# Cross attention: the exponentials cast to f16 and transposed by DMA, and their sums taken from a column of ones

## The chip, the cores and the metric

One core of one Trainium2 chip runs the whole kernel. The core's engines are TensorE (PE in the profile; PEld is its weight load), VectorE (DVE), ScalarE (ACT), GpSimd (POOL) and SyncE (SP), which only issues transfers here. The metric is device time in microseconds (us), from the launch of the program to its end; the profile's span runs from the first to the last instruction. Less is better.

## What is computed

The input `x` has 4 sequences of 2048 positions and 512 features, `ctx` 4 sequences of 128 positions. Three blocks follow each other, each as `x + block(layernorm(x))`:

```python
x = x + _L0_attn_ref(_layernorm(x), ...)    # 16 heads; attention over the 4 sequences of one position
x = x + _L0_xattn_ref(_layernorm(x), ctx_1024, ctx_1024, mask, ...)
x = x + _L0_ffn_ref(_layernorm(x), ...)
```

The change concerns the second one, cross attention with 16 heads of 32 features:

```python
scores = jnp.einsum('bnlh,bnph->bnlp', qm, km) / np.sqrt(HEAD_DIM)
scores = jnp.where(mask, scores, MASK_FILL)
attn = jax.nn.softmax(scores, axis=-1)
out = jnp.einsum('bnlp,bnph->bnlh', attn, vm)
return out @ Wo.T + bo
```

The third block, in the kernel a hinge function on a projection to 64 gates and a product back to 512 features, is interleaved with it. Inputs and outputs are f32.

## The kernel before

The program has two stages. `first_block` runs self attention over the positions and prepares the context: keys, mask and values go to memory in the form that the second stage reads. `cross_block` does cross attention and the third block. An f32 product is made from two parts, a high and a low one: ScalarE copies the source to the narrower type (high), VectorE subtracts this from the source (low), and TensorE multiplies high by high, high by low and low by high (`PASSES`). For the values' product the parts are f16, elsewhere `F32R`.

The cross stage has 16 steps (`step(j, p)`, run by `run_steps`) of 512 rows. A step has four tiles of 128 rows, numbered t = 0 to 3, and then the products that belong to all 512 rows: `ffn_in` for the step before and `queries` for the step to come. Each engine has its own hand-written order of work in its `step`, and semaphores tie them together; no scheduler moves anything. The work is staggered: in tile t TensorE computes the scores of tile t, but the values, the output projection and the rest belong to tiles one to three earlier.

One tile's way through attention, with the names of the code:

- `scores(t)` on TensorE: 4 products with `ones` and `fillrows` for the mask, 48 with the queries and `kt`, into the four banks `sc`.
- `tops(t, g)` on VectorE: the negative maximum of each head into `ntop`, four heads (one g) at a time.
- `exps(t, g)` on ScalarE: one exponential for each head into `prob` (f32, `prob_c` in the profile), with the head's sum by `accum_out`, which the profile shows as a second instruction, ACTIVATION_READ_ACCUMULATOR.
- `prob_T(i)` on TensorE: four heads of `prob` transposed into a bank of the ring; `prob_hi` and `prob_lo` on ScalarE and VectorE take the high and low part into `pT` (f16).
- `values(t)` on TensorE, a tile later: 48 products of `pT` with `v_c`, 32 columns each.
- `normalise(t)` on VectorE: the reciprocal of the sums and `attn` = values times reciprocal.
- `attn_T`, `attn_hi`, `attn_lo`: `attn` transposed, high and low part into `aT`.
- `out_proj(t)` on TensorE with `wo`; `add_attn(t)` on VectorE adds the residual `xr` into `x2`; `statistics(t)` takes mean and variance (`mv`, `vare`).
- `norm2(j, t)` on GpSimd: `rstd`, the normalised rows `xn2` and the addition of `bf`; then `norm2_T`, `norm2_hi`, `norm2_lo` into `x2T`, `ffn_in`, the hinges `g_sb`, the gates `gT` and `ffn_out`.

Beside this, GpSimd normalises the next step's rows (`norm(i)`, which waits for the load of `x1`) and adds the bias to the residual (`residual(i)`).

Transposes and most products write to a ring of four PSUM banks. `slot_turns` lists who takes a bank, in the order of TensorE's work, and `bank_before` gives the turn four places earlier, which must have been emptied (`taken`) before the bank is used again. SyncE's queue holds the loads of `x1`, of the rows of `kt`, `fillrows` and `v_c`, and the stores of the output.

## Time and profile before

| | |
|---|---|
| median of 3 runs | 1782.91 us (1781.09 to 1783.93) |
| the profiled execution | 1784.44 us |
| its span | 1782.6 us |
| PE busy | 1685.4 us (95%) |
| PEld busy | 1392.6 us (78%) |
| DVE busy | 1514.8 us (85%) |
| ACT busy | 1069.8 us (60%) |
| POOL busy | 1017.6 us (57%) |
| mean granted clock of TensorE | 0.983 |
| DMA | 98.75 MB, mean 55 GB/s |

The profiled execution takes 1.5 us more than the median. Around its span there are 1.8 us. The self stage fills the span up to about 844 us, the cross stage the rest. Busy times are sums over stages with different limits, so the table alone doesn't tell what holds a step. In the rows by stretch the columns are the length, then busy time and count of PE, PEld, DVE, ACT and POOL, the granted clock (1.00 is full), the DMA engines' busy share and GB/s; in the rows of a timeline they are the start, the duration, engine, line, operation with output and inputs, and in brackets the idle time before and what ended it. The rows are taken from one step in the middle of the cross stage (about 1206 to 1263 us), from its first tiles, and, for shapes that the cross stage doesn't have, from the self stage.

### The profile page before, as it was taken

What the parts mean: (1) busy time and instruction counts of PE and PEld (TensorE: products, weight loads), DVE (VectorE), ACT (ScalarE), POOL (GpSimd) and SP (SyncE); (2) the same over time, 40 slices, a digit from 0 to 9 for tenths busy, and PEclk for the clock granted to TensorE, in tenths of its full rate; (3) what the DMA queues carried; (4) which work ended last, traced back from release to release, by engine and by line L of the source; (5) the groups of instructions that cost most, each with busy time, mean ns of one, the idle gap of its engine ahead of it and who ended that gap; (6) DMA issues with size and microseconds to landing.
All of it is one profiled execution on the core that took longest, in us unless ns stands there. A gap on an engine that the chain in (4) does not pass through costs nothing.

```text
span 1782.6 us, 37666 instructions
## 1 busy us (share of the span) xinstructions
PE 1685.4 (95%) x13824; PEld 1392.6 (78%) x13824; DVE 1514.8 (85%) x2089; ACT 1069.8 (60%) x3420; POOL 1017.6 (57%) x721
## 2 busy tenths in 40 slices
PE   6899999999999999997799999999999999999996
PEld 5678888888888888885677787778777787777874
DVE  6788888888888888787678898888988899888886
ACT  4434444444443334442767788777877788777884
POOL 3267766666666666695554464545654465544521
PEclk9999999999999999998799999999999999999998
DMA  5410111111111111044201112011111112011101
GB/s 210 128 42 25 47 48 48 47 47 47 47 47 47 47 47 47 2 107 79 68 8 51 62 62 63 25 62 62 63 38 43 62 62 69 19 62 62 39 20 54
DMA packets 72793, 98.75 MB, mean 55 GB/s; under 512 B 22208, under 2 KB 30528, under 8 KB 72640
## 3 DMA queue, kind: packets, MB, share of 16 engines
q1 hardware_dynamic: 72064, 96.63, 17.0%
q8 instruction: 97, 1.59, 0.4%
q14 instruction: 56, 0.46, 0.1%
q10 hardware_dynamic: 576, 0.07, 0.0%
HBM read 59.66 MB, written 37.03 MB: 54 GB/s over the span
## 4 chain that ended last, share of the span: by engine, by line
PE 28%; ACT 12%; DVE 8%; issue 4%; DVEq 0%; POOL 0%; ACTq 0%; POOLq 0%
PE ring L1464 11%; ACT prob_c L1679 10%; DVE g_sb L1794 5%; PE sc L1492 5%; PE ring L1504 3%; PE ring L1469 3%; PE ring L1549 3%; PE sc L1484 2%; PE sc L1464 1%; DVE q_first L1975 1%; ACT relu L1660 1%; DVE g_sb L1791 1%; DVE gT L1803 1%; ACT gT L1669 1%; ACT pT L1648 0%
## 5 line engine op out<-in xcount | busy, mean ns | idle before, releaser
L447 PE MATMUL qb<-wqkv,xT 128*128 128x512 f32 x2304 | 551.9, 393 | 6.1 <-DVE wqkv L1016 6.1
L447 PEld LDWEIGHTS qb<-wqkv,xT 128*128 128x128 f32 x2304 | 429.7, 189 | 93.7 <-DVE wqkv L1016 6.3
L1679 ACT ACTIVATE prob_c<-sc,ntop 128x128 f32<-128x128 f32 x1024 | 362.6, 390 | 22.1 <-DVE ntop L1821 18.7
L1410 POOL TENSOR_TENSOR rstd<-vare,half_c 128x1 f32<-128x1 f32 x64 | 35.1, 549 | 433.6 <-DVE vare L1875 433.6
L1679 ACT ACTIVATION_READ_ACCUMULATOR prob_c<-sc,ntop 128x1 f32 x1024 | 236.1, 231 | 0.0
L352 POOL TENSOR_TENSOR prod_pool<-v,prob 128x1024 f32<-128x1024 f32 x64 | 179.9, 2810 | 67.8 <-DVE prob L911 62.6
L1464 PE MATMUL ring<-wqkv,aT_c 128*128 128x512 f32 x768 | 194.5, 402 | 8.0 <-DVE aT_c L1778 7.1
L663 ACT ACTIVATE v<-qb 128x512 f32<-128x512 f32 x64 | 38.3, 598 | 259.9 <-PE qb L447 249.6
L583 PE MATMUL ob<-wout,aT 128*128 128x512 f32 x768 | 191.4, 398 | 0.8 <-DVE aT L941 0.8
L1821 DVE TENSOR_REDUCE ntop<-sc 128x4 f32<-128x512 f32 x256 | 173.3, 683 | 12.3 <-PE sc L1492 9.5
L663 ACT ACTIVATE qk<-qb 128x512 f32<-128x512 f32 x128 | 76.1, 595 | 175.8 <-PE qb L447 175.8
L1778 DVE TENSOR_TENSOR pT<-ring,pT 128x512 f16<-128x512 f32 x256 | 172.0, 682 | 8.8 <-ACT pT L1648 8.8
L1464 PEld LDWEIGHTS ring<-wqkv,aT_c 128*128 128x128 f32 x768 | 139.3, 188 | 49.4 <-DVE aT_c L1778 20.0
L1464 PE MATMUL ring<-xT_c,wqkv 128*128 128x512 f32 x720 | 172.3, 398 | 0.0
L583 PEld LDWEIGHTS ob<-wout,aT 128*128 128x128 f32 x768 | 141.5, 189 | 29.4 <-DVE aT L941 1.0
L1464 PEld LDWEIGHTS ring<-xT_c,wqkv 128*128 128x128 f32 x720 | 134.5, 188 | 31.8 <-DVE xT_c L1778 0.2
L1504 PE MATMUL ring<-ident,prob_c 128*128 128x128 f32 x1024 | 142.4, 278 | 6.3 <-ACT prob_c L1679 5.9
L1648 ACT ACTIVATE pT<-ring 128x512 f16<-128x512 f32 x256 | 141.6, 624 | 0.1
L1504 PEld LDWEIGHTS ring<-ident,prob_c 128*128 128x128 f32 x1024 | 117.6, 144 | 16.3 <-ACT prob_c L1679 9.2
L849 DVE TENSOR_TENSOR prod<-qk 128x512 f32<-128x512 f32 (+1 forms) x64 | 129.6, 2025 | 0.3
L372 POOL TENSOR_TENSOR rstd<-vare,half 128x4 f32<-128x4 f32 x16 | 16.3, 1020 | 189.0 <-DVE vare L877 189.0
L1794 DVE SCALAR_TENSOR_TENSOR g_sb<-relu,hinge,g_sb 128x512 f32<-128x512 f32 x112 | 107.0, 956 | 6.8 <-DVE g_sb L1791 0.5
(152 smaller groups left out, 3358.5 us busy)
## 6 DMA issues: line engine op xcount, KB each, us to landing
x_tile<-in_x SPq DMA_DIRECT2D x16, 1024.0 KB, 5.2
x_scratch<-xres SPq DMA_DIRECT2D x16, 1024.0 KB, 4.6
x_tile<-x_scratch SPq DMA_DIRECT2D x16, 1024.0 KB, 5.3
out<-x SPq DMA_DIRECT2D x64, 256.0 KB, 2.0
kt<-k_scratch SPq DMA_DIRECT2D x16, 512.0 KB, 3.2
v_c<-v_scratch SPq DMA_DIRECT2D x16, 256.0 KB, 3.6
raw<-in_wqkv SPq DMA_DIRECT2D x3, 1024.0 KB, 8.9
ctx<-in_ctx SPq DMA_DIRECT2D x1, 1024.0 KB, 8.3
```

The lines of the kernel that those rows point to most:

```text
L352: nc.gpsimd.tensor_tensor(prod_pool[:, :, :].rearrange("p s (h d) -> p (s h) d", d=DH), v[:, s:s + 2, :].rearrange("p s (h d) -> p (s h) d ...
L447: last = nc.tensor.matmul(qb[g % 4][:, :], xT[p][a][:, k, t * P:(t + 1) * P], wqkv[b][:, k, c * D:(c + 1) * D], start=(n == 0), stop=(n == ...
L583: last = nc.tensor.matmul(ob[t % 2][:, :], aT[t % 2][a][:, k, :], wout[b][:, k, :], start=(n == 0), stop=(n == 11))
L663: nc.scalar.activation(dst, qb[g % 4][:, :], ACT.Copy, scale=SCALE if c == 0 else 1.0).then_inc(qkv_sb, 1)
L849: nc.vector.tensor_tensor(prod[:, 0:n, :], qk[:, 1, 0:n, :], qk[:, 0, t:t + 1, :].to_broadcast([P, n, D]), ALU.mult).then_inc(qk_mul, 1)
L1464: last = nc.tensor.matmul(dst, s, m, start=(n == 0), stop=(n == len(terms) - 1))
L1504: last = nc.tensor.transpose(dst[:, h * P:(h + 1) * P], prob[:, 4 * g + h, :], ident[:, :])
L1648: nc.scalar.activation(dst, ring[bank_of(j, (kind, i))][:, :], func, **kw).then_inc(hi[kind], 1)
L1679: last = nc.scalar.activation(prob[:, h, :], sc[g][:, (h % 4) * C:(h % 4 + 1) * C], ACT.Exp, bias=ntop[:, h:h + 1], accum_out=total[:, t % ...
L1778: nc.vector.tensor_tensor(dst, src, hi_part, ALU.subtract).then_inc(taken[kind], 1)
L1794: nc.vector.scalar_tensor_tensor(out=g_sb[:, :], in0=relu[:, i % 4, :], scalar=hinge[:, 2, i:i + 1], in1=g_sb[:, :], op0=ALU.mult, op1=ALU ...
L1821: nc.vector.tensor_reduce(ntop[:, 4 * g:4 * g + 4], sc[g][:, :].rearrange("p (h c) -> p h c", c=C), AX.X, ALU.max, negate=True).then_inc(t ...
```

## The change

The f32 exponentials are no longer transposed by TensorE. ScalarE casts them to f16 as they lie (`prob_hi(t, part)`, eight heads at a time, into `p16[0]`), GpSimd takes the low part of heads 0 to 7 and VectorE that of heads 8 to 15 (`prob_lo(t)`, into `p16[1]`), and SyncE transposes each of these four quarters (high and low, eight heads each, 128x1024 f16, 256 KB) by a DMA transpose from `p16` into `pT`. `pT` has two buffers, for the tile being multiplied and the next. The values get a column of ones behind each head (and a column of zeros, `VW` = 34), so that `values` gives 33 columns for each head and the last one is the head's sum; `accum_out` goes, and the reciprocal reads the ring. As 16 x 33 columns don't fit a bank, `values` takes two banks of the ring, and `banks_before` now gives the turns of both. `aT` and `gT` move into free columns of the buffers `wqkv` to make room.

The core of the diff; what is left out are the allocations, the loads and stores of the wider values in the first stage, and the removed calls of `prob_T`, `prob_hi` and `prob_lo`:

```diff
+            def turn(j, t, part):
+
+                n = 4 * j + t
+                heads = slice(8 * part, 8 * part + 8)
+                for h in range(2):
+                    if h == 0:
+                        wait(sp, p_hi, 2 * n + part + 1)
+                    else:
+                        wait(sp, p_lo[part], n + 1)
+                    wait(sp, psum["pv"], n - 1)
+                    sp.dma_start_transpose(pT[n % 2][h][:, heads, :],
+                                           p16[h][:, heads, :].rearrange("p h c -> p (h c)")).then_inc(turned[h][part], 16)
...
+                for t in range(R):
+                    if t < 3 and active(j, "out", t):
                         store(j, p, t)
-                if has(j, 1):
-                    load_ctx(j + 1, 1 - p)
+                    if has(j):
+                        turn(j, t, 0)
+                    if t == 3 and has(j, 1):
+                        load_ctx(j + 1, 1 - p)
+                    if has(j):
+                        turn(j, t, 1)
+                    if t == 3 and active(j, "out", t):
+                        store(j, p, t)
...
+                def prob_lo(t):
+                    if not has(j):
+                        return
+                    n = 4 * j + t
+                    wait(pool, p_hi, 2 * n + 1)
+                    wait(pool, turned[1][0], 16 * n)
+                    nc.gpsimd.tensor_tensor(p16[1][:, 0:8, :], prob[:, 0:8, :], p16[0][:, 0:8, :],
+                                            ALU.subtract).then_inc(p_lo[0], 1)
...
-                    wait(pe, taken["pT"], 4 * over)
...
-                    dst = bank(j, ("pv", t))
+                    bank(j, ("pv", t))
+                    dst = value_sums(j, t)
                     for h in range(H):
-                        head = slice(head_of(h) * DH, (head_of(h) + 1) * DH)
+                        head = head_of(h)
+                        if h % 8 == 0:
+                            wait_each(pe, (turned[0][h // 8], 16 * over), (turned[1][h // 8], 16 * over))
                         for n, (a, b) in enumerate(PASSES):
-                            last = nc.tensor.matmul(dst[:, head], pT[a][:, h, :], v[:, pp, b, head],
+                            last = nc.tensor.matmul(dst[:, head // 8, head % 8, :], pT[(over + 1) % 2][a][:, h, :],
+                                                    v[:, pp, b, head, 0:DH + 1],
                                                     start=(n == 0), stop=(n == 2))
...
-                    wait(act, psum["pT"], 16 * j + 4 * t - 3 + g)
-                    if g == 0:
-                        wait(act, taken["pv"], 4 * j + t - 1)
+                    wait(act, p_lo[g // 2], 4 * j + t)
                     for h in range(4 * g, 4 * g + 4):
                         last = nc.scalar.activation(prob[:, h, :], sc[g][:, (h % 4) * C:(h % 4 + 1) * C],
-                                                    ACT.Exp, bias=ntop[:, h:h + 1],
-                                                    accum_out=total[:, t % 2, head_of(h):head_of(h) + 1])
+                                                    ACT.Exp, bias=ntop[:, h:h + 1])
...
+                def prob_hi(t, part):
+
+                    n = 4 * j + t
+                    heads = slice(8 * part, 8 * part + 8)
+                    wait(act, exped, 4 * n + 2 * part + 2)
+                    wait(act, turned[0][part], 16 * n)
+                    nc.scalar.activation(p16[0][:, heads, :], prob[:, heads, :], ACT.Copy).then_inc(p_hi, 1)
...
+                def prob_lo(t):
+
+                    n = 4 * j + t
+                    wait(dve, p_hi, 2 * n + 2)
+                    wait(dve, turned[1][1], 16 * n)
+                    nc.vector.tensor_tensor(p16[1][:, 8:, :], prob[:, 8:, :], p16[0][:, 8:, :],
+                                            ALU.subtract).then_inc(p_lo[1], 1)
```

Three places show what this does to the order of instructions. The first is VectorE between two middle tiles of a step, from the last instruction of `statistics` to `attn_lo` (`aT_c`, in the changed kernel a part of `wqkv`). Before:

```order
L1875 TENSOR_SCALAR vare<-mv 128x1
L1778 TENSOR_TENSOR x2T<-ring,x2T 128x4x128
L1778 TENSOR_TENSOR pT<-ring,pT 128x512
L1821 TENSOR_REDUCE ntop<-sc 128x4
L1778 TENSOR_TENSOR pT<-ring,pT 128x512
L1778 TENSOR_TENSOR aT_c<-ring,aT_c 128x512
```

After:

```order
L1907 TENSOR_SCALAR vare<-mv 128x1
L1859 TENSOR_TENSOR p_1<-prob_c,p_0 128x1024
L1808 TENSOR_TENSOR x2T<-ring,x2T 128x4x128
L1851 TENSOR_REDUCE ntop<-sc 128x4
L1808 TENSOR_TENSOR wqkv<-ring,wqkv 128x4x128
```

Two passes of 128x512 have gone, and one of 128x1024 (`p_1` is `p16[1]`, `p_0` is `p16[0]`) stands ahead of the rest.

The second is VectorE in the last tile of a step, from `attn_lo(3)` to `normalise(3)` (`xT_c` is the next step's normalised input, `xr` marks `add_attn`). Before:

```order
L1778 TENSOR_TENSOR aT_c<-ring,aT_c 128x512
L1821 TENSOR_REDUCE ntop<-sc 128x4
L1778 TENSOR_TENSOR xT_c<-ring,xT_c 128x4x128
L1778 TENSOR_TENSOR pT<-ring,pT 128x512
L1821 TENSOR_REDUCE ntop<-sc 128x4
L1778 TENSOR_TENSOR pT<-ring,pT 128x512
L1861 TENSOR_TENSOR x_0<-ring,xr 128x512
L1778 TENSOR_TENSOR xT_c<-ring,xT_c 128x4x128
L1821 TENSOR_REDUCE ntop<-sc 128x4
L1850 TENSOR_TENSOR x_0<-ring,x_0 128x512
L1883 RECIPROCAL rtotal<-total_c 128x16
```

After:

```order
L1808 TENSOR_TENSOR wqkv<-ring,wqkv 128x4x128
L1851 TENSOR_REDUCE ntop<-sc 128x4
L1808 TENSOR_TENSOR xT_c<-ring,xT_c 128x4x128
L1851 TENSOR_REDUCE ntop<-sc 128x4
L1808 TENSOR_TENSOR xT_c<-ring,xT_c 128x4x128
L1851 TENSOR_REDUCE ntop<-sc 128x4
L1893 TENSOR_TENSOR x_0<-ring,xr 128x512
L1882 TENSOR_TENSOR x_0<-ring,x_0 128x512
L1916 RECIPROCAL rtotal<-ring 128x16
```

`add_attn` stands behind the second `xT_c` and the last maxima now, where it was ahead of both, and by the ring's turns `values(3)` waits for it.

The third is GpSimd around a step's start, from the last `norm2` of a step to that of the next one's first tile. Before:

```order
L1410 TENSOR_TENSOR rstd<-vare,half_c 128x1
L1415 TENSOR_TENSOR xn<-x_1,mv 128x512
L1419 TENSOR_TENSOR xn<-xn,rstd 128x512
L1420 TENSOR_TENSOR x_1<-x_1,bf 128x512
L1392 TENSOR_TENSOR xn_c<-x_tile,st_c 128x512
L1395 TENSOR_TENSOR xn_c<-xn_c,st_c 128x512
L1392 TENSOR_TENSOR xn_c<-x_tile,st_c 128x512
L1395 TENSOR_TENSOR xn_c<-xn_c,st_c 128x512
L1410 TENSOR_TENSOR rstd<-vare,half_c 128x1
```

After:

```order
L1471 TENSOR_TENSOR rstd<-vare,half_c 128x1
L1476 TENSOR_TENSOR xn<-x_1,mv 128x512
L1480 TENSOR_TENSOR xn<-xn,rstd 128x512
L1481 TENSOR_TENSOR x_1<-x_1,bf 128x512
L1444 TENSOR_TENSOR xn_c<-x_tile,st_c 128x512
L1447 TENSOR_TENSOR xn_c<-xn_c,st_c 128x512
L1444 TENSOR_TENSOR xn_c<-x_tile,st_c 128x512
L1447 TENSOR_TENSOR xn_c<-xn_c,st_c 128x512
L1461 TENSOR_TENSOR p_1<-prob_c,p_0 128x1024
L1471 TENSOR_TENSOR rstd<-vare,half_c 128x1
```

The low part of the step's first tile stands behind `norm(0)` and `norm(1)`, which wait for the load of `x1`, and ahead of the next `norm2`.

## Rows read from the trace of the kernel before

**Rows 1.** Busy time by stretch: a middle tile, the last with queries, the first
```profile
1206.43:1216.34 9.91, 9.66 (x141) 8.05 (x141) 9.42 (x18) 8.73 (x39) 6.34 (x6) 1.00 0.08 29
1216.34:1244.65 28.31, 27.57 (x226) 22.36 (x226) 24.83 (x39) 21.84 (x60) 15.23 (x14) 1.00 0.25 77
1244.65:1253.51 8.86, 7.94 (x129) 6.89 (x128) 7.54 (x14) 6.38 (x34) 0.00 (x1) 1.00 0.09 33
```

**Rows 2.** Timeline of TensorE in that middle tile: start, duration, instructions
```profile
1208.64 1.04 PE L1504 MATMUL ring<-ident,prob_c 128*128 128x128 f32 x8
1209.60 0.96 PE L1464 MATMUL ring<-wqkv,gT 128*128 128x512 f32 x3
1210.40 3.02 PE L1464 MATMUL ring<-wqkv,aT_c 128*128 128x512 f32 x12
1213.36 1.37 PE L1549 MATMUL ring<-v_c,pT 128*128 128x32 f16 x48
```

**Rows 3.** Timeline of VectorE from one `attn` to the next
```profile
1205.03 0.69 DVE L1887 TENSOR_TENSOR attn_c<-ring,rtotal 128x512 f32<-128x512 f32 x1
...
1206.58 0.15 DVE L1875 TENSOR_SCALAR vare<-mv 128x1 f32<-128x1 f32 x1
...
1208.86 0.68 DVE L1778 TENSOR_TENSOR pT<-ring,pT 128x512 f16<-128x512 f32 x1
1209.54 0.69 DVE L1778 TENSOR_TENSOR aT_c<-ring,aT_c 128x512 fp32r<-128x512 f32 x1
...
1214.94 0.69 DVE L1887 TENSOR_TENSOR attn_c<-ring,rtotal 128x512 f32<-128x512 f32 x1
```

**Rows 4.** Timeline of TensorE and VectorE: last tile, queries, `attn` of the next tiles
```profile
1224.30 1.36 PE L1549 MATMUL ring<-v_c,pT 128*128 128x32 f16 x48
...
1226.50 0.69 DVE L1887 TENSOR_TENSOR attn_c<-ring,rtotal 128x512 f32<-128x512 f32 x1
...
1230.98 11.49 PE L1464 MATMUL ring<-xT_c,wqkv 128*128 128x512 f32 x48
...
1249.24 0.69 DVE L1887 TENSOR_TENSOR attn_c<-ring,rtotal 128x512 f32<-128x512 f32 x1
...
1262.03 0.69 DVE L1887 TENSOR_TENSOR attn_c<-ring,rtotal 128x512 f32<-128x512 f32 x1
```

**Rows 5.** Timeline of ScalarE: two copies, an exponential, its sum, the next
```profile
1210.76 1.10 ACT L1648 ACTIVATE pT<-ring 128x512 f16<-128x512 f32 x2
...
1213.77 0.45 ACT L1679 ACTIVATE prob_c<-sc,ntop 128x128 f32<-128x128 f32 x1
1214.02 0.30 ACT L1679 ACTIVATION_READ_ACCUMULATOR prob_c<-sc,ntop 128x1 f32 x1
1214.11 0.46 ACT L1679 ACTIVATE prob_c<-sc,ntop 128x128 f32<-128x128 f32 x1
```

**Rows 6.** Groups by line and shape, self stage (100 to 700 us): busy, mean ns
```profile
L930 DVE TENSOR_TENSOR prod<-prod 128x1024 f32<-128x1024 f32 x26 | 65.2, 2509 | 0.9
...
L849 DVE TENSOR_TENSOR prod<-qk 128x1024 f32<-128x1024 f32 x13 | 15.8, 1215 | 0.0
...
L352 POOL TENSOR_TENSOR prod_pool<-v,prob 128x1024 f32<-128x1024 f32 x52 | 147.4, 2836 | 47.3 <-DVE prob L911 42.8 <-POOL attn L362 2.2
```

**Rows 7.** Timeline of GpSimd at the end of that tile, behind the statistics
```profile
1206.81 0.55 POOL L1410 TENSOR_TENSOR rstd<-vare,half_c 128x1 f32<-128x1 f32 x1 [2.13 <-DVE vare L1875]
```

**Rows 8.** Timelines in the first step: exponentials of the second tile, first `norm`
```profile
858.68 0.37 ACT L1679 ACTIVATE prob_c<-sc,ntop 128x128 f32<-128x128 f32 x1 [3.09 <-DVE ntop L1821]
...
861.48 1.04 POOL L1392 TENSOR_TENSOR xn_c<-x_tile,st_c 128x512 f32<-128x512 f32 x1 [6.36 <-DMA st_c<-st_scratch]
```

**Rows 9.** DMA issues of 256 KB: count, size, median us from issue to landing
```profile
out<-x SPq DMA_DIRECT2D x64, 256.0 KB, 2.0
...
v_c<-v_scratch SPq DMA_DIRECT2D x16, 256.0 KB, 3.6
```

**Rows 10.** Timeline of TensorE near the end of the self stage
```profile
827.38 1.12 PE L455 MATMUL tb<-ident,attn 128*128 128x128 f32 x4 [2.43 <-DVE attn L934]
```

More of the change, by code:

```diff
@@ L1207, in active @@
 def active(j, kind, i):
[L1209 removed]
+    shift = {"pv": -(i == 0), "aT": -(i < 2), "wo": -(i < 2), "x2T": -(i < 3),
              "xT": 1, "q": 1, "s": -1, "out": -2}[kind]
@@ L1223, with ring_places @@
 RING = [(j, kind, i) for j in range(TILES) for kind, i in TURNS
-        if active(j, kind, i) and (j, kind, i) not in ENDING] + ENDING
-PLACE = {turn: n for n, turn in enumerate(RING)}
+        if (j, kind, i) not in ENDING] + ENDING
+def ring_places():
+    place, user, n = {}, {}, 0
+    for turn in RING:
+        width = 2 if turn[1] == "pv" else 1
+        if n % 4 + width > 4:
+            n += 1
+        place[turn] = n
+        for at in range(n, n + width):
+            user[at] = turn
+        n += width
+    return place, user
+PLACE, USER = ring_places()
 def bank_of(j, turn):
@@ L1235, in head_of, with banks_before @@
     return 4 * (slot % 4) + slot // 4
-def bank_before(j, turn):
-    at = PLACE[(j, *turn)] - 4
-    if at < 0:
-        return None
-    step, kind, i = RING[at]
-    return kind, TURNS_OVER[kind](step, i)
-CROSS_SMALL = [("kt", [P, 2, DK, C], F32R), ("fillrows", [P, C], F32R), ("v_c", [C, 2, 2, D], F16),
+def banks_before(j, turn):
+    first = PLACE[(j, *turn)]
+    found = []
+    for at in range(first, first + (2 if turn[0] == "pv" else 1)):
+        at -= 4
+        while at >= 0 and (at not in USER or not active(*USER[at])):
+            at -= 4
+        if at >= 0 and USER[at] not in found:
+            found.append(USER[at])
+    return [(kind, TURNS_OVER[kind](step, i)) for step, kind, i in found]
+CROSS_SMALL = [("kt", [P, 2, DK, C], F32R), ("fillrows", [P, C], F32R), ("v_c", [C, 2, 2, H, VW], F16),
                ("bo", [P, D], F32), ("bf", [P, D], F32), ("hinge", [P, 3, PAIRS], F32), ("bin", [P, 1], F32),
@@ L1453, in bank @@
             def bank(j, turn):
-                before = bank_before(j, turn)
-                if before:
-                    wait(pe, taken[before[0]], before[1])
+                for kind, over in banks_before(j, turn):
+                    wait(pe, taken[kind], over)
                 return ring[bank_of(j, turn)]
@@ L1495, in scores @@
                                     last.then_inc(scored, 1)
-                def prob_T(i):
-                    if not has(j):
-                        return
-                    g = i % 4
-                    wait(pe, exped, 16 * j + i + 1)
-                    dst = bank(j, ("pT", i))
-                    for h in range(4):
-                        last = nc.tensor.transpose(dst[:, h * P:(h + 1) * P], prob[:, 4 * g + h, :], ident[:, :])
-                    last.then_inc(psum["pT"], 1)
                 def attn_T(t, j=j):
```

165 lines of the change are left out of this document (67 added, 98 removed).

## The prediction

> **What bounds the kernel now.** I read first the busy times by stretch, then the timelines of the engines over one step, and last the groups of like instructions. The self stage (up to about 844 us) stays as it is but for a few small instructions on the context's values, costed at nothing: its tensor products hide them. The cross stage is 16 steps of 512 rows, each with four tiles of 128 rows. In the middle tiles TensorE is busy 9.66 of 9.91 us and VectorE 9.42, and 27.57 of 28.31 us in the long stretch with the query products [rows 1]. Two engines that are both full usually hold each other in a ring, so I look for the ring. [rows 2] and [rows 3] show it. VectorE writes `attn` (1205.03), takes statistics (the last at 1206.58), does four passes of 0.60 to 0.75 us, then the low part of `aT` (1209.54); only then may TensorE do the output projection (1210.40) and the values (1213.36), and only behind these comes the next `attn` (1214.94). That is 9.91 us from one `attn` to the next. The eight transposes of exponentials lie beside this ring (1208.64 to 1209.60), while TensorE would wait for `aT` anyway. So the 0.96 us that eight of them take doesn't become shorter tiles by itself. The distances from `attn` to `attn`, with the last rows, are 9.91, 11.56, 22.74 and 12.79 us, in sum 57.0 us a step [rows 2, 4].
>
> **What goes, and what of it counts.** TensorE loses 64 transposes a step, 8 x 0.96 = 7.7 us. ScalarE loses the 0.09 us behind each exponential (0.34 from one to the next becomes 0.25, [rows 5]), 16 x 0.09 = 1.4 us a tile, and four copies of 0.48 us a tile (two take 1.10, of which the last 0.62 is its own, [rows 5]). VectorE loses four passes of 0.60 a tile. Of all this only what lies on the ring counts: the two passes between statistics and `aT`, 1.35 us.
>
> **What comes.** ScalarE gets two copies of 128x1024 a tile. From the rows (0.25 us for 128 columns, 0.48 for 512) I take 0.9 us each. VectorE gets one subtraction of 128x1024 from SBUF with an f16 result, and it stands straight behind the statistics, ahead of `x2T`, the maxima and `aT`: inside the ring. The trace has the shape in f32 at both ends: 1.22 us where GpSimd is not at work, 2.51 us where it is [rows 6]. GpSimd starts its own normalising passes at just that moment, since the same statistics release it (0.23 us behind, [rows 7]): first a tiny one of 0.55 us, then 128x512 passes. So I take 1.7 us in the middle tiles (0.65 us undisturbed, the rest at half speed), nearer to the low end, and 2.1 in the first tile, where it starts later and meets more of them. GpSimd gets the same for the other eight heads, 2.8 us by the nearest row [rows 6]; it lies between passes that nobody waits for soon, except in the first step. The Trainium skill (VectorE: DVE Perf Modes, Mode 2x_1P) says that a two-input pass goes at double rate only if all its operands have 16 bits; here one is f32. By that page the 1.2 us stays and 0.6 us is not to be had; no row shows an f16 input, so the trace is silent.
>
> **The sum, distance by distance.**
> Second to third tile: the statistics end 1.67 us behind `attn`; then 1.7 (low part), 0.6 (`x2T`), 0.6 (maxima), 0.7 (`aT` with its hand-over), 0.14 to the projection, 2.96 for it, 1.3 for the values, and now the reciprocal too, since the sums come out of the same product: 0.45 with its waits. In sum 10.1 for 9.91: +0.2.
> Third to fourth: here the values' product needs two banks, and one of them was last used by the projection of the same tile. So it waits for the addition that empties it, and VectorE has that behind the second `xT` low part and the last maxima. From `aT` (5.3 behind `attn`): projection and the `xT` transposes 3.6, ScalarE's copy 0.85, `xT` low part 0.6, maxima 0.6, addition 0.7, then values, reciprocal and hand-over 1.6: 13.2 for 11.56, +1.6. Before, the values began at 1224.30, 0.8 us behind that projection's end [rows 4].
> Fourth to the next step's first: four groups of transposes go, but the queries now start behind statistics 1.6, low part 1.7, two `xT` low parts 1.2 and a hand-over: 4.6 us behind `attn`, where they were 4.48 behind [rows 4]. The queries' 11.3 us and VectorE's hinges behind them stay. One pair of transposes at their end goes, mostly into a wait for the gate: -0.2.
> First to second: here the low part waits for ScalarE's second copy, no longer for the statistics. The first tile's stretch was 8.86 us long [rows 1] and ended with the exponentials. So counted from its scores' start: 8.86 - 0.3 for the hand-over - 5.4 + 4.0 for the shorter exponentials + 0.9 for the copy among them + 0.4 for a maximum that now comes late + 0.9 + 0.15 for the copy behind = 9.5. Then 2.1 + 0.6 + 0.6 + 0.7 + 0.14 + 2.96 + 1.3 + 0.45, less the 4.6 at which `attn` stands (1249.24 behind 1244.65): 13.8, and 0.3 for a last transpose that comes late: 14.1 for 12.79, +1.3.
> A step: 57.0 + 0.2 + 1.6 - 0.2 + 1.3 = 59.9 us. Fifteen repeats give 15 x 2.9 = 43.5 us.
> First step, once: the exponentials of the second tile now wait for GpSimd's low part of the first. In GpSimd's queue this stands behind two normalisings, and they wait for a load: the first ran at 861.48 [rows 8], four passes of about 1.05, then 2.8 gives 868.5, where the exponentials ran at 858.68 [rows 8]: +9.8 us. In later steps that load is long there.
> The profiled execution took 1784.4 us (span 1782.6): 1784.4 + 43.5 + 9.8 = 1837.7. The median of the three runs is 1.5 lower, so I forecast **1836 us**.
>
> **Bounds of the unknown prices.** A low part of 1.2 us throughout takes away 0.5 + 0.9 + 0.5 + 0.5 = 2.4 us a step: 1800. At 2.5 us throughout it adds 0.8 + 0.4 + 0.8 + 0.8 = 2.8: 1878. If exponentials don't get shorter without their sums, the first tile gains nothing: +1.4 a step, 1857. The transposes by DMA have no row. As plain transfers of 256 KB they would land after 2.0 to 3.6 us [rows 9]. From the end of the low part to the values that read it there are 0.6 + 0.6 + 0.7 + 0.14 + 2.96 = 5.0 us, so up to 5 us are hidden by the projection; each us beyond is paid in every tile. I take them as hidden.
>
> **Rivals.**
> *The DMA transposes become the bound.* Sixteen of them a step stand in one queue, four for each tile. In the middle tiles there are 10.1 us for four, so the point is 2.5 us of queue time each. At 3.6 us (the slow row of [rows 9] taken as occupancy) a tile needs 14.4 us: at least 0.3 + 4.3 + 1.2 a step, 1930; as the last of the four can't start before the low part, about as much again, 2020. At 6 us each the queue alone needs 96 us a step: about 2400. For: stores and row loads stand in the same queue, and nothing shows a transpose's rate. Against: the 80 transfers of that size in [rows 9] land fast. The Trainium skill speaks on both sides. Its page DMA: Bandwidth & Descriptors (Latency and other measured facts) has 261 GB/s for a DMA transpose, by which a quarter takes 1.0 us and is hidden; its page VectorE: DVE Perf Modes (The three transpose paths) has 1309 ns for one 128x128 block, by which eight in a row take 10.5 us, and the step 168. No row here decides between them.
> *The freed time arrives (the other side).* If the f16 subtraction ran at twice the rate of the f32 row, 0.6 us, each distance would shrink by 1.1 to 1.5 us: 5.0 a step, 54.9, and with the first step 1784.4 - 31.5 + 9.8 - 1.5 = 1761. The point is about 0.85 us. The utmost, TensorE's 7.7 us a step all saved, would be 1784.4 - 123 = 1661; for that the low part would have to leave the ring, and the order of instructions holds it there.
> *TensorE's clock.* A wait of 2.43 us in the change of stages was followed by four transposes in 1.12 us, where eight take 1.04 [rows 10, 2]: the clock had gone to the lower of its two levels (1.2 GHz). In the new ring `aT` comes 5.7 us behind the values' end, and TensorE has 3.6 us of work until then (transposes 0.5, scores 1.8, transposes 0.5, gate product 0.8): a wait of 2.1 us in each tile. If the clock falls in each, projection and values lengthen by some 1.5 us: 3 x 1.5 x 16 = +72, 1908. Against: the wait is shorter than the one seen, and the engine is dense around it.
> *The change doesn't do what it says:* that exponentials still cost 0.34 us is in the bounds above.
>
> **How the numbers follow.** Forecast with its bounds (1795 to 1880) 0.54; transposes or clock in between (1880 to 2080) 0.20; transposes at several us each (above 2080) 0.12; faster by over 0.2%, 0.11; within 0.2% (about what this kernel's measurement can tell from no change) 0.03. The likeliest time is 1836. The range 1785 to 2080 leaves out the faster cases and the slowest, 0.23 together. Slower: 0.54 + 0.20 + 0.12 = 0.86.
>
> **What would show it.** Right: `attn` to `attn` of about 14, 10, 13 and 22.5 us; VectorE's low part at 1.5 to 2.1 us straight behind the statistics; TensorE idle about 2 us ahead of each projection, released by VectorE's `aT`; in the fourth tile the values released by VectorE's addition; GpSimd in the first step waiting for the load while ScalarE waits for it; ScalarE busy far less. Wrong: the values waiting for a DMA (then the transposes' time decides); low parts under 0.85 us; granted clock under 1.00 in the steady steps; a step shorter than 57 us, which would mean that the ring I read is not the one that holds.

## The result, and the profile after

The kernel after takes **1848.94 us** (median of 5 runs, 1832.45 to 1851.72), the kernel before 1782.91: ratio 1.0351, 95% interval 1.033 to 1.0372. It is slower by 66 us. The forecast was 1836, in the range 1785 to 2080. Its sum comes out near the time, and that nearness is in good part luck: the longer ring that I priced at 43 us costs some 3 to 15, and TensorE's clock, which I had as a rival with no term in the sum, pays most of the rest.

The profiled execution is the fastest of the five, with a span of 1830.6 us against 1782.6. Its page, by engine and in 40 slices:

```profile
PE 1604.9 (88%) x12800; PEld 1311.5 (72%) x12800; DVE 1434.2 (78%) x1899; ACT 997.0 (54%) x2268; POOL 1218.4 (67%) x785
...
PEclk9999999999999999996789898989999999999998
```

TensorE is busy 80.5 us less than before, VectorE 80.6, ScalarE 72.8, GpSimd 200.8 more. Nothing of what the two fullest engines save comes out as time. In the steady steps TensorE's clock is no longer full. By stretch (length, busy us of PE, PEld, DVE, ACT, POOL, granted clock, DMA share, GB/s), where every stretch of [rows 1] had 1.00:

```profile
1000.00:1700.00 700.00, 588.60 (x6683) 476.23 (x6682) 539.26 (x862) 485.54 (x1144) 497.74 (x379) 0.95 0.59 122
1180.00:1240.00 60.00, 51.50 (x568) 41.17 (x566) 45.34 (x73) 40.06 (x95) 41.46 (x32) 0.91 0.62 119
```

VectorE's timeline from an `attn` on, which answers to [rows 3]:

```profile
1245.23 0.69 DVE L1919 TENSOR_TENSOR attn_c<-ring,rtotal 128x512 f32<-128x512 f32 x1
...
1246.77 0.15 DVE L1907 TENSOR_SCALAR vare<-mv 128x1 f32<-128x1 f32 x1
1246.85 1.22 DVE L1859 TENSOR_TENSOR p<-prob_c,p 128x1024 f16<-128x1024 f32 x1
...
1249.19 0.68 DVE L1808 TENSOR_TENSOR wqkv<-ring,wqkv 128x512 fp32r<-128x512 f32 x1
```

The low part takes 1.22 us, not 1.7. So the low part of `aT` (printed as `wqkv`, in whose free columns it lies) comes 3.96 us behind `attn`, where it was 4.51 [rows 3]: this part of the ring got shorter. TensorE in the same stretch, with its idle time ahead in brackets:

```profile
1240.60 3.01 PE L1529 MATMUL ring<-wqkv 128*128 128x512 f32 x12 [1.60 <-DVE wqkv L1808]
...
1249.92 4.62 PE L1529 MATMUL ring<-wqkv 128*128 128x512 f32 x12 [1.57 <-DVE wqkv L1808]
...
1257.63 1.36 PE L1605 MATMUL ring<-v_c,pT 128*128 128x33 f16 x48 [1.95 <-issue]
```

The same projection took 3.02 us before [rows 2] and takes 3.01 and then 4.62 here, behind waits of 1.60 and 1.57. 4.62 us is a projection of which a good part ran at the lower of the two levels. The distances from `attn` to `attn`, mean of the 14 steps behind the first (in brackets the median, which the longest slow stretches move less):

| us | 1st to 2nd | 2nd to 3rd | 3rd to 4th | 4th to 1st | step |
|---|---|---|---|---|---|
| before | 12.80 (12.78) | 9.89 (9.91) | 11.53 (11.57) | 22.69 (22.73) | 56.91 |
| forecast | 14.1 | 10.1 | 13.2 | 22.5 | 59.9 |
| after | 14.07 (13.45) | 9.44 (9.33) | 13.19 (12.69) | 22.64 (22.59) | 59.34 |

Before, 13 of the 14 steps lie between 56.5 and 57.2 us; after, they run from 57.9 to 62.1. The first `attn` of the cross stage is at 874.35, 10.14 us later than before (864.21). From there to the same tile fifteen steps on it is 38.06 us more, and the rest 0.2 less: 10.1 + 38.1 - 0.2 = 48.0, the difference of the spans. The other four runs were 14 to 19 us longer still, with a mean clock of 0.942 to 0.944 in place of 0.952.

### The profile page after: what moved, and what is told of

The parts are those of the page before. It is cut to its first block, busy times and chain, and to the rows that moved or that the text cites. A ratio compares the mean times of both kernels' runs of the same rounds, so it can differ in the third digit from the quotient of the medians.

```text
span 1830.6 us, 34906 instructions
## 1 busy us (share of the span) xinstructions
PE 1604.9 (88%) x12800; PEld 1311.5 (72%) x12800; DVE 1434.2 (78%) x1899; ACT 997.0 (54%) x2268; POOL 1218.4 (67%) x785
## 4 chain that ended last, share of the span: by engine, by line
PE 63%; DVE 18%; issue 8%; ACT 6%; DMA 2%; SPq 1%; POOL 1%; DVEq 0%; ACTq 0%; POOLq 0%
PE qb L452 25%; PE ring L1529 17%; PE ob L588 9%; PE ring L1605 3%; PE tb L460 3%; ACT prob_c L1720 3%; DVE wqkv L1808 2%; PE ring L1534 2%; DVE ntop L1851 2%; PE sc L1529 2%; DVE x2T L1808 2%; DVE stats L1902 2%; DVE g_sb L1824 1%; PE sc L1557 1%; DVE xT_c L1808 1%
## 5 line engine op out<-in xcount | busy, mean ns | idle before, releaser
L1529 PE MATMUL ring<-wqkv 128*128 128x512 f32 x960 | 282.3, 441 | 94.4 <-DVE wqkv L1808 71.6
L1720 ACT ACTIVATE prob_c<-sc,ntop 128x128 f32<-128x128 f32 x1024 | 286.5, 376 | 73.8 <-DVE ntop L1851 59.8
L1529 PEld LDWEIGHTS ring<-wqkv 128*128 128x128 f32 x960 | 192.3, 211 | 158.5 <-DVE wqkv L1808 92.0
L1461 POOL TENSOR_TENSOR p<-prob_c,p 128x1024 f16<-128x1024 f32 x64 | 136.8, 2137 | 139.2 <-ACT p L1730 139.2
L1730 ACT ACTIVATE p<-prob_c 128x1024 f16<-128x1024 f32 x128 | 135.4, 1058 | 4.0
L1605 PE MATMUL ring<-v_c,pT 128*128 128x33 f16 x3072 | 89.0, 179 | 46.9 <-issue 30.7
L1605 PEld LDWEIGHTS ring<-v_c,pT 128*128 128x128 f16 x3072 | 84.2, 97 | 62.3 <-issue 62.0
L1444 POOL TENSOR_TENSOR xn_c<-x_tile,st_c 128x512 f32<-128x512 f32 x60 | 72.0, 1200 | 78.6 <-DMA st_c<-st_scratch 78.6
L1471 POOL TENSOR_TENSOR rstd<-vare,half_c 128x1 f32<-128x1 f32 x64 | 77.1, 1205 | 70.6 <-DVE vare L1907 70.5
L1703 ACT ACTIVATE relu<-sc,hinge 128x512 f32<-128x512 f32 x128 | 92.3, 777 | 39.7 <-PE sc L1529 37.1
```

The lines of the kernel that those rows point to most:

```text
L1461: nc.gpsimd.tensor_tensor(p16[1][:, 0:8, :], prob[:, 0:8, :], p16[0][:, 0:8, :], ALU.subtract).then_inc(p_lo[0], 1)
L1529: last = nc.tensor.matmul(dst, s, m, start=(n == 0), stop=(n == len(terms) - 1))
L1605: last = nc.tensor.matmul(dst[:, head // 8, head % 8, :], pT[(over + 1) % 2][a][:, h, :], v[:, pp, b, head, 0:DH + 1], start=(n == 0), sto ...
L1703: nc.scalar.activation(relu[:, i % 4, :], sc[number][:, :], ACT.Relu, bias=hinge[:, 1, i:i + 1], scale=hinge[:, 0, i:i + 1]).then_inc(relu ...
L1720: last = nc.scalar.activation(prob[:, h, :], sc[g][:, (h % 4) * C:(h % 4 + 1) * C], ACT.Exp, bias=ntop[:, h:h + 1])
L1730: nc.scalar.activation(p16[0][:, heads, :], prob[:, heads, :], ACT.Copy).then_inc(p_hi, 1)
```

## The experiments

Eleven kernels ran, each beside the kernel before on the same chip; its medians there are 1782.9 to 1784.3 us. The ratio is to that median.

| kernel | median us | ratio (95%) | clock, profiled |
|---|---|---|---|
| after | 1848.94 | 1.0351 (1.0330 to 1.0372) | 0.952 |
| e1_fill | 1814.23 | 1.0171 (1.0154 to 1.0188) | 0.975 |
| e2_first | 1838.86 | 1.0317 (1.0296 to 1.0338) | 0.951 |
| e3_no_low | 1797.31 | 1.0071 (1.0047 to 1.0095) | 0.954 |
| e4_bank | 1818.45 | 1.0191 (1.0174 to 1.0208) | 0.955 |
| e5_move | 1855.65 (1829.31 to 1865.88) | not given, too uneven | 0.939 |
| e6_accum | 1900.85 | 1.0678 (1.0640 to 1.0716) | 0.930 |
| v2_order | 1888.69 | 1.0592 (1.0572 to 1.0611) | 0.931 |
| v1_order_fill | 1888.20 | 1.0583 (1.0553 to 1.0614) | 0.942 |
| v3_order | 1789.99 | 1.0032 (1.0015 to 1.0049) | 0.963 |
| v4_order_fill | 1780.76 | 0.9996 (0.9977 to 1.0015) | 0.969 |
| v5_fill_more | 1769.81 | 0.9924 (0.9907 to 0.9940) | 0.980 |

**Is it the clock?** In the kernel after, TensorE gets work without use in its waits, in steps 1 to 14: `count` is 5 ahead of each output projection and 6 ahead of `values(3)`.

```
+    for _ in range(count):
+        nc.tensor.matmul(dst, wo[0][:, 0, 0:P], wo[0][:, 0, :], start=True, stop=True)
...
     wait(pe, taken["aT"], TURNS_OVER["wo"](j, t))
```

> The kernel after, with work for TensorE in its waits in steps 1 to 14: five products of 128x512 (about 1.2 us) into the bank of the output projection ahead of each wait for `aT`, and six ahead of the fourth tile's values, into the values' first bank; the real products overwrite them. Theory clock: of the 66 us that the kernel after costs by the medians, about 25 are the longer ring and first step (steps of 58.0 us where no product is slow, against 57.0, and 10 us once), and the rest is TensorE at its lower clock behind waits of 1.3 to 2 us. Then the filled kernel shows a granted clock of 1.00 in the steady steps, steps of 58 us, and 1784 + 15 + 10 = about 1810 us, ratio to before about 1.015. Theory ring (the clock is beside the point, the distances are long by VectorE and GpSimd alone): the time stays at about 1849, or rises by up to 1 us a tile (64 tiles, 1910) where the added products end later than the wait did.

Measured: 1814.23, near the 1810 of the clock. The stretches, and TensorE ahead of a projection and of the fourth tile's values (L1581 is the work without use):

```profile
1000.00:1700.00 700.00, 651.67 (x7267) 527.34 (x7266) 553.99 (x891) 500.93 (x1187) 517.64 (x393) 1.00 0.61 127
...
1234.44 1.41 PE L1581 MATMUL ring<-wqkv 128*128 128x512 f32 x5
1236.28 3.03 PE L1529 MATMUL ring<-wqkv 128*128 128x512 f32 x12 [0.43 <-DVE wqkv L1818]
...
1242.40 1.36 PE L1615 MATMUL ring<-v_c,pT 128*128 128x33 f16 x48 [0.56 <-issue]
```

The clock of the steady steps is 1.00 again, and the step shrinks from 59.34 to 57.42 us with more work in it. Added work made the kernel 35 us faster by the medians (25 us between the profiled executions). In these steps the ring is 12.96, 9.33, 12.57 and 22.30 us (medians): 57.2, against 57.0 before. With the clock held, the new ring is as long as the old one to within 0.2 us. Of the 22.9 us by which this profiled span exceeds the one before, 9.7 lie ahead of the first `attn`, 5.7 in the first step, which has none of the added work and still runs slow products, and 7.2 in the 14 others, 2.3 of them in the one that still has slow products.

**The first step.**

```
+                if is_step(j, 0):
+                    prob_lo(0)
                 if has(j, 1):
                     wait(pool, x1_in, 32 * (j + 2))
```

> The kernel after, with GpSimd's low part of the first tile put ahead of the two normalisings in the first step alone. If the first step's 10 us are ScalarE's exponentials waiting for that low part behind the x1 load, the first `attn` mark comes back from 874.35 to about 864 and the time falls by 10 us: 1839, ratio 1.029. Rival: the late normalisings then hold the fourth tile's transposes of that step, or the first values wait for their DMA anyway, and the gain is under 3 us: 1846 to 1849.

ScalarE's timeline in the first step, of the kernel after and then of this one:

```profile
867.10 2.18 ACT L1720 ACTIVATE prob_c<-sc,ntop 128x128 f32<-128x128 f32 x8 [12.29 <-POOL p L1461]
```

```profile
858.43 2.17 ACT L1723 ACTIVATE prob_c<-sc,ntop 128x128 f32<-128x128 f32 x8 [3.20 <-DVE ntop L1854]
```

The exponentials are back where they were (858.68, [rows 8]), so their cause is shown. But the first `attn` comes at 867.30, not at 864: now the values wait 6.06 us for their DMA, whose first transpose could issue at 857.99 only, behind the load of the next rows. 7.05 of the 10.14 us come back at that place. The medians differ by 10 us, the ratios by 0.34%, or 6 us, with intervals that overlap; the two profiled executions are equal, since this one lost 7 us in slow products later.

**Is the low part on the ring?** From the second step on VectorE's low part takes 2 of the 128 columns of each head; the kernel leaves out the rest.

```
-    nc.vector.tensor_tensor(p16[1][:, 8:, :], prob[:, 8:, :], p16[0][:, 8:, :],
+    part = slice(0, C if j == 0 else 2)
+    nc.vector.tensor_tensor(p16[1][:, 8:, part], prob[:, 8:, part], p16[0][:, 8:, part],
```

> The kernel after, with VectorE's low part cut from 128 to 2 columns of each head from the second step on (1.2 us becomes about 0.1; the low parts of these heads are stale, so their values lose precision; nothing else changes, the waits and DMA transposes stay). Theory on the ring: the pass stands between statistics and `aT` low part, so each distance shrinks by up to 1.1 us, in the middle tiles down to TensorE's own work of about 8.7: steps of 58.0 - 0.6 - 1.0 - 1.1 - 1.1 = 54.2, TensorE's waits go and its clock stays at 1.00: 1784 + 10 - 15 x 2.8 = about 1752, ratio 0.983. Rival beside the ring (TensorE waits for ScalarE's `aT` or for the exponentials as long): steps stay at 58 and more, the time above 1835.

The three steps of the 14 in which no product is slow take 54.4 to 54.8 us, about as worked out (54.2), and each of their four distances is shorter than in the kernel after. So the pass is on the ring in all four. But the time is 1797, not 1752: the other steps have slow products and take up to 59.0 us, since TensorE still waits:

```profile
1234.70 3.01 PE L1529 MATMUL ring<-wqkv 128*128 128x512 f32 x12 [1.04 <-DVE wqkv L1808]
...
1240.81 1.36 PE L1605 MATMUL ring<-v_c,pT 128*128 128x33 f16 x48 [1.96 <-issue]
```

The theory had the clock return once the ring is short; that was wrong.

**The fourth tile's banks.**

```
                 out_proj(3)
+                values(3)
                 norm_T(1)
                 ffn_out(3)
-                values(3)
```

In the ring of banks `("pv", 3)` moves behind `("wo", 3)` likewise, and the copies and low parts of `xT` 1 behind the values on ScalarE and VectorE.

> The kernel after, with the fourth tile's values put straight behind its projection, into two banks of which neither is the projection's; the second `xT` transposes and the gate product follow them, and so do their copies on ScalarE and VectorE. Theory bank: the distance third to fourth tile falls from 12.6 to about 9.33 + 0.6 (one more group of transposes) + 0.6 (one more low part) = 10.5 us, of which the queries behind it give about half back since `xT` comes later; 16 x 1 to 2 us = 16 to 32 us, and the slow projection of that tile goes too (some 10 to 20 us): 1800 to 1825. Rival: the queries' start is what counts, and it waits for four `xT` whichever way the values go: the distance fourth to first grows by what the third to fourth loses, 1845 to 1855.

Measured: 1818.45, inside the range. The third distance falls from 12.69 to 9.3 us, more than worked out, and the long one grows from 22.6 to 24.6, since the queries now wait:

```profile
1198.48 11.51 PE L1529 MATMUL ring<-xT_c,wqkv 128*128 128x512 f32 x48 [1.57 <-DVE xT_c L1808]
```

The net is 1.3 us a step, 57.9 to 56.6 in the shortest ones: 20 of the 30 us. The wait of 1.95 us ahead of the values is gone. The other 10 us go with the clock: its mean over an execution is 0.942 in the median one of the kernel after and 0.955 to 0.957 in all four of this kernel. That the wait of 1.95 us had brought them is argued, not shown.

**Are the transposes hidden?** VectorE's low part behind `aT` and the second maxima, in the fourth tile behind the last `xT`.

```
-                    prob_lo(t - 1)
                     norm2_lo(t - 1)
                     tops(t, 0)
                     attn_lo(t)
                     tops(t, 1)
+                    prob_lo(t - 1)
```

> The kernel after, with VectorE's whole low part out of the ring: in each tile it stands behind the `aT` low part and the second maxima in place of ahead of `x2T`, and that of the fourth tile behind the last two `xT` low parts. Theory place: what costs is where the pass stands. The distances fall as they did when the pass was cut to 2 columns (8.7, 12.0, 21.4, 12.7 undisturbed), but its DMA transposes now start some 2 us behind the `aT` low part and land 3.2 us later, while the values come 3.1 us behind it: each middle tile's values wait about 2 us for a DMA, so the middle distances come back to 9.9 to 10.7 and only the long one gains (1.2 us): steps of about 58 us, time 1835 to 1855, with the values now released by DMA. Rival: the transposes land in time and the time is that of the cut pass, about 1800.

Between 1829 and 1866, in the middle 1856, just above what was expected, and the trace shows the wait that was expected, TensorE at the second half of the values:

```profile
1239.13 3.02 PE L1529 MATMUL ring<-wqkv 128*128 128x512 f32 x12 [0.77 <-DVE wqkv L1808]
1242.00 0.77 PE L1605 MATMUL ring<-v_c,pT 128*128 128x33 f16 x24
1244.03 0.76 PE L1605 MATMUL ring<-v_c,pT 128*128 128x33 f16 x24 [1.27 <-DMA pT<-p]
```

`attn` to `attn` in this tile is 9.9 us, longer than with the pass inside the ring (9.33); with slow products it is up to 13.5, and 11.0 at the median. The quiet long distance falls to 21.5, but the first grows from 13.35 to 14.6, where 12.7 was expected; why, I did not follow. In the kernel after the transposes are hidden (from 1000 to 1700 us TensorE's only idle time ahead of values is the 1.95 us of the fourth tile), in this one they aren't, and the difference is where the pass stands, not what it costs. The transposes of the kernel after by the DMA view from 900 to 1700 us (count, median us to landing):

```profile
pT<-p SPq DMA_TRANSPOSE x212, 3.2
```

In SP's queue, here of the v2_order below, two issues behind each other take 3.13 us, so four in a tile of 9.3 us, some 6.3 us, leave it room:

```profile
1200.76 3.13 SPq L1405 DMA_TRANSPOSE pT<-p  x2
```

**Do the sums cost ScalarE again what they did?** The exponentials get `accum_out` into a spare tile.

> The kernel after, with the exponentials writing their sums again (into a spare tile that nobody reads), 64 x 16 of them. This undoes the one saving that lies on ScalarE. Each exponential should again take 0.34 us from one to the next in place of 0.26, 1.3 us a tile. Theory of the prediction: it counts where ScalarE's exponentials end a wait, the first tile of each step (scores of the second tile wait 1.47 us for them): +1.3 us a step, +20, 1869. Rival: it counts in the other tiles too, where TensorE waits 0.2 us for the same exponentials ahead of each scores: up to 4 x 1.3 x 16 = +80, 1930; or not at all, if the low part on VectorE hides it: within 5 us of 1849.

Measured: 1900.85, 52 us more, between the two. Start to start of the exponentials in this kernel is 0.35 us:

```profile
1180.95 0.35 ACT L1721 ACTIVATE prob_c<-sc,ntop 128x128 f32<-128x128 f32 x1
1181.20 0.19 ACT L1721 ACTIVATION_READ_ACCUMULATOR prob_c<-sc,ntop 128x1 f32 x1
1181.30 0.36 ACT L1721 ACTIVATE prob_c<-sc,ntop 128x128 f32<-128x128 f32 x1
```

In the kernel after eight take 2.16. The first distance goes from 13.35 to 14.8 us where it is least slowed (+1.4, the prediction's size), and the second not at all. The third takes 14.38 us in the two of the 14 steps where the clock is full from the second `attn` to the fourth, 1.7 more than 12.7. (It is 12.9 only behind a second distance that slow products had made 12.5.) There VectorE's low part no longer follows the statistics but waits for ScalarE's second copy, and then runs into GpSimd's passes:

```profile
1207.17 1.75 DVE L1860 TENSOR_TENSOR p<-prob_c,p 128x1024 f16<-128x1024 f32 x1 [0.96 <-ACT p L1731]
```

So the sums cost about 3 us a step, some 46 in all, and count in the third distance too, which the prediction's bound of +1.4 a step leaves out. The rest is slow products: 15.8 to 16.1 us in the third distance or 16.2 in the first, in nearly every step. TensorE at the second tile's scores, whose 48 products take 1.45 us elsewhere:

```profile
1246.75 0.74 PE L1550 MATMUL sc<-fillrows,ones 32*128 32x512 f32 x4 [2.56 <-ACT prob_c L1721]
1247.28 2.67 PE L1558 MATMUL sc<-kt,q_first 32*128 32x128 f32 x48
```

A wait that grew from 1.47 to 2.56 us cost twice: once itself, once in the clock behind it.

**All of it together, at first wrongly.** v2_order is e2_first, e4_bank and e5_move, with `ffn_out(t)` behind `out_proj(t)` in the middle tiles.

> Everything that the first experiments found, together, on the kernel after: GpSimd's first low part ahead of its normalisings in the first step (-10); fourth tile's values behind its projection in free banks; VectorE's low parts out of the ring as in e5_move; and the gate product of the middle tiles moved between projection and values, so that TensorE has 0.8 us of work while the transposes land. Theory place: middle distances of 8.9 to 9.4, fourth 9.3, long one 24.6 - 1.2 = 23.4, first to second 12.7: 54.8 a step; 1784 - 15 x 2.2 = 1751 if the clock holds, 1775 to 1790 if it falls in the waits as before. Rival: the DMA transposes land too late for that and each middle tile stays at 10: 56 to 57 a step, 1790 to 1805.

Measured: 1888.69, 100 us above the expectation, which falls. The quiet middle tile is 11.14 us and the quiet fourth 11.3, not 9. In a middle tile the second half of the values waits 0.94 us for its transpose (at 1184.65) and the next scores 0.80 for ScalarE's exponentials. In a fourth tile:

```profile
1193.39 0.77 PE L1608 MATMUL ring<-v_c,pT 128*128 128x33 f16 x24
1195.98 0.76 PE L1608 MATMUL ring<-v_c,pT 128*128 128x33 f16 x24 [1.82 <-DMA pT<-p]
```

Here the values wait 1.82 us for the DMA. The low part stands amid GpSimd's passes there and takes 1.60 us (from 1191.00), and from its end to the product that reads it are 3.4 us. Moreover the slow products came in nearly every step; that the gate product, which no longer stands ahead of the projection, had kept them off is not shown, since four changes went in together. With filling it is no better:

> v2_order with five products of 128x512 without use ahead of each output projection (about 1.2 us of TensorE's time each, steps 1 to 14), as in e1_fill. With the low part out of the ring and the gate product moved behind the projection, TensorE waits 1.2 to 1.6 us there, so the fill should fit. If the clock is what is left: v2_order less some 15 to 25 us, about 1755 to 1765, granted clock near 1.00. If the wait ahead of the projection is shorter than the fill: up to 1 us a tile more than v2_order, and the clock no different.

Measured: 1888.20. The work without use stood ahead of the projection, and the wait for the DMA was inside the values (0.53 us in a middle tile, at 1188.86, and 1.25 in the fourth, at 1203.03).

**Together without that move.** v3_order keeps the middle tiles' low parts in the ring, and moves only the fourth's:

```
+                norm_lo(2)
+                norm_lo(3)
                 prob_lo(3)
-                norm_lo(2)
-                norm_lo(3)
```

> The parts that paid alone, without the move of the middle tiles' low part that made the values wait for their DMA: first step's low part ahead of the normalisings (e2_first), fourth tile's values behind its projection (e4_bank), and new: in the fourth tile the last two `xT` low parts ahead of the probabilities' low part, whose DMA has the whole query product to land in. The queries waited 1.57 us for `xT` in e4_bank, behind a low part of 2.1 us: they start up to 2 us earlier. Distances 9.3, 9.3, 22.6 to 23.4, 13.4: steps of 54.9 to 55.4 us where no product is slow, 1784 - 15 x 1.8 = about 1757 undisturbed. Theory clock: waits of 1.3 to 1.6 us ahead of every projection are still there, so it loses 25 to 35 us to slow products: 1782 to 1792, ratio 1.00. Rival (the slow products came with the long waits of the fourth tile only): about 1760.

> v3_order with five products of 128x512 without use ahead of each output projection in steps 1 to 14, as in e1_fill. Theory clock: most of what v3_order loses comes back, 1757 plus 5 to 10 us: 1762 to 1770, ratio 0.99, faster than the kernel before. Rival: as v3_order or slower.

> v4_order_fill with five more such products at each of the two other places where TensorE waits 1.3 to 1.5 us once a step: ahead of the first gate product (it waits for VectorE's low part of the gate) and ahead of the second tile's scores (they wait for the first tile's exponentials). Theory clock: the falls that e1_fill still had (0.975 in place of 0.98 and more) lie behind these two; 3 to 8 us less than v4_order_fill. Rival: they fit no wait and cost up to 2 x 1 us a step, up to 30 us more.

v3_order: 1789.99, as the clock's theory had it, with quiet steps of 55.4 us (13.34, 9.34, 9.30, 23.40). v4_order_fill: 1780.76, better by 9 us and 11 to 19 short of the expectation. Its trace says where the rest is. The wait for the gate's low part grew to 2.20 us in this order, and the scores behind it run slow, 2.52 us in place of 1.46:

```profile
1184.49 0.95 PE L1532 MATMUL ring<-wqkv 128*128 128x512 f32 x3 [2.20 <-DVE wqkv L1843]
...
1185.71 2.52 PE L1560 MATMUL sc<-kt,q_first 32*128 32x128 f32 x48
1188.16 1.11 PE L1537 MATMUL ring<-ident,attn_c 128*128 128x128 f32 x4
```

v5_fill_more fills this wait too (`idle_work(bank(j, ("out", 0)), 5)` ahead of `ffn_out(0)`, and five ahead of the second tile's scores): **1769.81 us**, 11 us less than v4_order_fill, where 3 to 8 were expected, ratio 0.9924. It beats both kernels. Whether the new order of the fourth tile would make the kernel before faster too, no run tells, so this doesn't show that the transposes by DMA pay. Its clock from 1000 to 1700 us is 1.00, its steps are 55.2 to 56.4 us:

```profile
1000.00:1700.00 700.00, 672.34 (x7431) 546.42 (x7429) 577.98 (x915) 509.69 (x1210) 513.35 (x396) 1.00 0.63 130
```

## Why the prediction came out, point by point

**The bound and the ring: right.** The ring through `aT`, projection, values and `attn` holds the time before and after; e3_no_low and e4_bank each shorten it where they should.

**Second to third tile, +0.2 forecast, -0.6 measured in the median (-0.45 in the mean): wrong in sign.** The step that failed is the price of VectorE's low part, "so I take 1.7 us in the middle tiles (0.65 us undisturbed, the rest at half speed)". It is 1.22. The two engines don't share by halves: the one that comes first runs at its full speed, and the other stands still until it is done. In the middle tile VectorE comes first, and GpSimd's small pass of 0.55 us [rows 7] takes 1.48 instead:

```profile
1247.00 1.48 POOL L1471 TENSOR_TENSOR rstd<-vare,half_c 128x1 f32<-128x1 f32 x1 [0.24 <-DVE vare L1907]
```

In the first tile GpSimd comes first, here by the timelines of both engines:

```profile
1344.19 1.04 POOL L1476 TENSOR_TENSOR xn<-x,mv 128x512 f32<-128x512 f32 x1
```

```profile
1344.69 1.62 DVE L1859 TENSOR_TENSOR p<-prob_c,p 128x1024 f16<-128x1024 f32 x1 [1.10 <-ACT p L1730]
```

GpSimd's pass lasts until 1345.2, and VectorE's, from 1344.69, takes 1.62 us: 0.4 of standing and 1.2. In e1_fill the addition came 0.65 us later, GpSimd's passes with it, and the same low part took 1.23; that is the 0.4 us by which its first distance is shorter. The Trainium skill (SBUF — State Buffer, Who interferes with whom) says that the pair of ports which the two share is an exclusive lock, and that a VectorE instruction with two SBUF inputs contends with a GpSimd instruction that reads SBUF. The trace agrees with its 1.22, 1.48 and 1.62 us, and I should have priced by it.

The groups of [rows 6] were misread as well. I took their 1.22 us for VectorE where GpSimd is not at work. The timelines of the kernel before have GpSimd at work in both cases. The two start together, and GpSimd takes 3.00 us where it takes 2.11 elsewhere (at 299.72):

```profile
303.62 1.22 DVE L849 TENSOR_TENSOR prod<-qk 128x1024 f32<-128x1024 f32 x1
303.61 3.00 POOL L352 TENSOR_TENSOR prod_pool<-v,prob 128x1024 f32<-128x1024 f32 x1
```

Or GpSimd is long under way, until 336.7, and VectorE takes the 1.74 us until then and most of its own 1.22:

```profile
334.95 2.82 DVE L930 TENSOR_TENSOR prod<-prod 128x1024 f32<-128x1024 f32 x1
332.75 3.94 POOL L352 TENSOR_TENSOR prod_pool<-v,prob 128x1024 f32<-128x1024 f32 x1 [3.57 <-DVE prob L911]
```

So the order of the two was there to be read, and with it the 1.22 us of the middle tiles.

**Third to fourth, +1.6 forecast, +1.1 measured in the median (+1.7 in the mean): mechanism right, size off.** The values wait 1.95 us and follow the addition; e4_bank shows it. The 0.5 between is the low part again.

**Fourth to first, -0.2 forecast, -0.1 measured in the median.** Near by two errors: with the low part 0.5 us cheaper it should have been -0.7. The queries do start earlier, 4.10 us behind `attn` in place of 4.46, wherever no product ahead of them is slow, and such distances are 22.0 to 22.6. But in about half of the steps they start 4.7 to 5.1 us behind, since products behind the values' wait of 1.95 us are slow, here the eight transposes, which take 1.07 us at full clock:

```profile
1316.25 1.95 PE L1534 MATMUL ring<-ident,xn_c 128*128 128x128 f32 x8
```

**First to second, +1.3 forecast, +0.2 to +0.6 measured without slow products.** The low part again, 1.62 or 1.23 us where I had 2.1. The mean with slow products is +1.3, the forecast's own figure, and that is luck.

So the ring's +2.9 us a step is +0.2 with the clock held and about +1.0 in the kernel after's quiet steps (58.0), of which the slow transposes just shown are a part: 3 to 15 us, not 43.5.

**First step, +9.8 forecast, +10.1 measured.** The exponentials ran at 867.10 where I had 868.5. Right in place and size; that 3 us of it stand behind a second wait, for the DMA, I had not seen.

**Transposes hidden: right.** 3.2 us to landing, of the 5 us that I counted as covered. The rivals of a transpose-bound queue fall. From the 261 GB/s that the Trainium skill (DMA: Bandwidth & Descriptors, Latency and other measured facts) has for a DMA transpose, a quarter would take 1.0 us, an estimate. From the 1309 ns that the Trainium skill (VectorE: DVE Perf Modes, The three transpose paths) has for one block of 128x128, it would take eight times as long, 10.5 us, an estimate too. The 3.2 us here lie between, and nearer to the first. From the pass to the product it took 3.4 us in v2_order, so the cover of 5 us had 1.6 to spare, and e5_move used it up.

**Exponentials without sums: right** (0.26 us measured, 0.25 forecast). ScalarE's copies are 0.97 us from one start to the next (0.9), GpSimd's low part 2.14 (2.8).

**TensorE's clock: the rival that mostly happened.** I had it at a wait of 2.1 us in each tile, and +72 us if it fell in each. The longer waits are 1.25 to 1.95, and it falls behind some of them: 25 us of the profiled 48 come back when the waits are filled, 35 of the 66 by the medians. I gave it no term in the likeliest sum, because the wait was shorter than the one seen and the engine dense around it [rows 10]. That reason failed: the shortest wait behind which products ran slow in the kernel after is 1.25 us, straight behind the queries, in which TensorE had been busy 11.44 of 12 us:

```profile
1036.69 0.96 PE L1529 MATMUL ring<-wqkv 128*128 128x512 f32 x3 [1.25 <-DVE wqkv L1833]
...
1037.91 1.85 PE L1557 MATMUL sc<-kt,q_first 32*128 32x128 f32 x48
```

Two of the prediction's own signs bear on this. "Granted clock under 1.00 in the steady steps" stood under wrong, and it is 0.95. The low part "at 1.5 to 2.1 us" stood under right, and it is 1.22 in three of the four tiles. The other signs came as forecast: the waits for `aT`, if of 0.3 to 1.6 us and not 2, the values released by the addition, and GpSimd's wait for the load.

The sum was thus 1784 + 10 (right) + 43 (should be 3 to 15) + 0 (should be 25 to 40). What stays open: some 10 us between the parts can't be given to ring or clock for certain, since only one of the five executions has a trace, the added work of e1_fill also shifts the other engines, and its first step has none. What makes one wait of 1.5 us be followed by slow products and the next not, no run tells.

## What to carry to other kernels

Taking work off a full engine doesn't shorten a ring that another step of it holds; it turns the work into waits, and TensorE's waits of 1.25 to 2.6 us can cost a second time in its clock, as they did here, so a removal there must be costed with the products behind the new wait at both levels. When VectorE and GpSimd meet in passes like these, price the one that comes first at its own speed and the other at that plus the rest of the first, and ask which of the two is on the path. Before moving a pass whose result goes through a DMA, count the time from its end to the reader: here it took 3.2 to 3.4 us, and the values of e5_move and v2_order waited up to 1.3 and 1.8 us of them.

## What I had not expected of the hardware

Products without use made the kernel faster, by 35 us in e1_fill and by 20 us in v5_fill_more against v3_order. The clock fell behind waits that are shorter than the one seen before: a projection of 4.62 us in place of 3.02 behind a wait of 1.57. A GpSimd instruction on 128x1 elements took 1.48 us in place of 0.55 while VectorE's low part ran beside it.
